# Narrow attention heads on quarters of the array, four heads' scores issued for two steps at once, and the copies of transposed probabilities moved to the front of a step

## What is computed

```python
x = ln(x + attn0(x))                    # 16 heads of 64, one extra key and value of zeros
x = ln(x + xattn0(x, ctx, mask))        # 16 heads of 16, keys with mask 0 are left out
x = ln(x + moe(x))                      # 8 experts, two per token
x = ln(x + ssm(x))                      # 4 layers of a selective scan
x = ln(x + xattn1(x, ctx))              # own block with 8 heads of 32, and a feed-forward part
x = ln(x + bitlinear_ffn(x))
```

## Time and profile before

| what | value |
|---|---|
| median of 3 runs | 4847.31 us (4841.17 to 4852.92) |
| profiled execution | 4848.16 us |
| its span | 4846.5 us |
| PE busy | 83% of the span |
| DVE busy | 65% |
| ACT busy | 48% |
| POOL busy | 47% |
| granted PE clock, mean | 0.935 |

### The profile page before, as it was taken

How to read it: one execution, slowest core, us unless ns; L and a number is a source line. 1 busy time by engine, 2 the same in 40 slices (tenths; PEclk the granted TensorE clock), 3 DMA queues, 4 the chain that set the end, 5 groups by cost and what they waited for, 6 DMA issues and landing times.

```text
span 4846.5 us, 47769 instructions
## 1 busy us (share of the span) xinstructions
PE 3999.0 (83%) x14984; PEld 2038.4 (42%) x14992; DVE 3135.2 (65%) x4273; ACT 2329.8 (48%) x4232; POOL 2281.4 (47%) x1206
## 2 busy tenths in 40 slices
PE   7888888888869995888888888888888966676766
PEld 3433443444449992233333333333333323333333
DVE  3555446446541112699999998999899995554454
ACT  4444445435422223666666666666666542232332
POOL 2344334324410004678777787778777773120210
PEclk9999999999979997899999999999999998887988
DMA  6000000000058882011111111111111120000000
GB/s 208 18 5 10 18 13 2 18 14 9 1 197 316 310 321 86 22 36 33 45 34 37 31 45 33 38 33 45 33 38 33 33 65 33 1 13 13 0 5 4
DMA packets 102370, 272.71 MB, mean 56 GB/s; under 512 B 9776, under 2 KB 55728, under 8 KB 96400
## 3 DMA queue, kind: packets, MB, share of 16 engines
q1 hardware_dynamic: 97216, 256.75, 15.6%
q0 software_dynamic: 4944, 13.51, 0.8%
HBM read 237.32 MB, written 32.90 MB: 56 GB/s over the span
## 4 chain that ended last, share of the span: by engine, by line
PE 54%; DVE 15%; POOL 15%; issue 11%; ACT 3%; SPq 1%; DMA 1%; DVEq 0%; POOLq 0%; ACTq 0%
POOL AR L706 10%; PE PS L1319 6%; PE PS L1112 6%; PE PS L1095 6%; PE PS L1083 6%; PE PS L1208 6%; PE PS L1059 5%; DVE AR L1760 5%; PE PS L1067 4%; PE PS L1264 4%; PE PS L1218 3%; DVE PS L1754 3%; PE PS L1235 2%; POOL AR L664 1%; ACT AR L769 1%
## 5 line engine op out<-in xcount | busy, mean ns | idle before, releaser
L706 POOL TENSOR_TENSOR AR<-AR 128x1024 f32<-128x1024 f32 x512 | 1212.7, 2370 | 520.5 <-DVE AR L1760 520.4
L605 POOL TENSOR_TENSOR AR<-AR,rden 128x1024 f32<-128x1024 f32 x320 | 605.7, 1893 | 1292.0 <-DVE rden L1523 1225.8
L1319 PE MATMUL PS<-AR,ident 128*128 128x512 f32 x2048 | 1034.4, 629 | 195.7 <-POOL AR L706 195.6
L1760 DVE TENSOR_TENSOR_SCAN AR<-AR,PS 128x1024 f32<-128x1024 f32 x512 | 1170.3, 2286 | 17.6
L968 ACT ACTIVATE AR<-AR,mcol 128x511 f32<-128x511 f32 x1024 | 664.9, 711 | 143.1 <-DVE AR L1760 139.5
L1754 DVE TENSOR_TENSOR PS<-AR,PS 128x1024 f32<-128x1024 f32 x512 | 627.9, 1226 | 143.3 <-PE PS L1305 127.7
L1319 PEld LDWEIGHTS PS<-AR,ident 128*128 128x128 f32 x2048 | 367.6, 194 | 680.3 <-issue 341.4
L1095 PE MATMUL PS<-ident,AR 128*128 128x128 f32 x2560 | 345.2, 278 | 124.4 <-issue 67.1
L1095 PEld LDWEIGHTS PS<-ident,AR 128*128 128x128 f32 x2560 | 276.8, 142 | 383.7 <-issue 363.5
L1083 PE MATMUL PS<-AR 64*128 64x512 f32 x1280 | 365.0, 651 | 52.0 <-ACT AR L769 23.0
L769 ACT ACTIVATE AR<-PS,nm 128x512 f32<-128x512 f32 x384 | 260.1, 683 | 282.2 <-DVE nm L1503 217.0
(11 more groups left out here) (265 smaller groups left out, 4798.3 us busy)
## 6 DMA issues: line engine op xcount, KB each, us to landing
AR<-in_xw SPq DMA_DIRECT2D x39, 3072.0 KB, 10.4
AR<-mid_cs SPq DMA_DIRECT2D x256, 256.0 KB, 3.3
mid_xs<-AR SPq DMA_DIRECT2D x32, 512.0 KB, 8.0
AR<-mid_xs SPq DMA_DIRECT2D x39, 128.0 KB, 9.5
mid_ys<-AR POOLq DMA_DIRECT2D x39, 128.0 KB, 8.0
AR<-in_ctx SPq DMA_DIRECT2D x8, 512.0 KB, 5.1
AR<-in_mask SPq DMA_DIRECT2D x4, 1024.0 KB, 5.2
mid_x<-AR SPq DMA_DIRECT2D x8, 512.0 KB, 3.0
```

The costliest lines, as they stand in the source:

```text
L605: pool.tensor_tensor(probs[:, i % 4], probs[:, i % 4], rden[:, i % 4, :].rearrange("p (q o) -> p q o", o=1).to_broadcast([P, 2, 512]), ALU ...
L706: pool.tensor_tensor(m_HC[:, W % 3], m_H[:, W % 3, :].rearrange("p (c s) -> p c s", c=2), m_cb[:, n % 4:n % 4 + 1, :].to_broadcast([P, 2, ...
L1319: ins = pe.matmul(PS[:, 2 * hf + c, :], ident[:], m_HC[:, W % 3, c, :], start=False, stop=n == NS - 1)
L1760: v.tensor_tensor_scan(m_H[:, W % 3, :], m_dA[:, W % 4].rearrange("p c s -> p (c s)"), PS[:, 4:6, :].rearrange("p c s -> p (c s)"), 0.0, A ...
```

## The change

For `per` = 4 each head gets its own quarter of the array. The projected queries are kept once, so `pj_q`, the second copy and the small tables behind it go. One step still takes two heads, but the order of steps alternates between two pairs of heads, so that steps i and i+1 (i even) hold the four heads of a block for the same queries. PE issues the scores of both steps together, in even steps only, as four matmuls with 32 rows each into four PSUM banks. Before them it waits for step i-1: in B for its `nm` (`smax`), in E for its exponentials (`probs_ok`). AV goes to four matmuls of 256 moving columns on four column quarters, in place of two of 512. In `per` = 4 both DVE and ACT issue the copy of T(i-3) as the first thing of step i. Attention A keeps its order.

```diff
         def head(j, q, per):
-            return 2 * j + q if per == 2 else 4 * (j // 2) + j % 2 + 2 * q
+            return 2 * j + q
+
+        def step_of(i, per):
+            return (i // T, i % T) if per == 2 else (2 * (i // 8) + i % 2, i % 8 // 2)
...
# ACT
                 for i in range(n + LAG):
+                    if i >= LAG and per == 4:
+                        copy(i - LAG)
                     if i < n:
+                        exps(i)
+                    if i >= LAG and per == 2:
+                        copy(i - LAG)
...
                 for c in range(4):
-                    pj_q(b, PJ_BQ + c, b_qT, c, 4, qs_b, qb_b)
+                    pj(b, PJ_BQ + c, b_qT[:, c, :], ACT.Identity, 0.25, cols[:, C_BQ + c:C_BQ + c + 1])
...
# PE
-                        if i >= 2:
-                            pe.wait_ge(probs_ok, s - 1)
-                        for q in range(2):
-                            h = head(i // T, q, per)
-                            r = 64 * q
-                            part = h % 2 * (qT.shape[1] // 2) if per == 4 else 0
-                            ins = pe.matmul(PS[:, 2 * (i % 2) + q, :],
-                                            qT[r:r + 64, part + h // per, t * P:(t + 1) * P],
-                                            kT[r:r + 64, h // per, :], start=True, stop=True)
-                        ins.then_inc(scores, 1)
+                        free = smax if masked else probs_ok
+                        if per == 2 and i >= 2:
+                            pe.wait_ge(probs_ok, s - 1)
+                        if per == 4 and i % 2 == 0 and i >= 2:
+                            pe.wait_ge(free, s)
+                        for e in ((i,) if per == 2 else (i, i + 1) if i % 2 == 0 else ()):
+                            j, t = step_of(e, per)
+                            for q in range(2):
+                                h = head(j, q, per)
+                                r = h % per * wide
+                                ins = pe.matmul(PS[:, 2 * (e % 2) + q, :], qT[r:r + wide, h // per, t * P:(t + 1) * P],
+                                                kT[r:r + wide, h // per, :], start=True, stop=True)
+                            ins.then_inc(scores, 1)
...
-                        for q in range(2):
-                            h = head(j, q, per)
-                            p0 = h % per * wide
-                            ins = pe.matmul(PS[p0:p0 + wide, 6 + bank % 2, :], V[:, c, h * wide:(h + 1) * wide],
-                                            pT[j % 2][:, q, c, :], start=c == 0, stop=c == 3)
+                        for q in range(per):
+                            h = per * bank + q
+                            p0 = q * wide
+                            n0 = 0 if per == 2 else u % 2 * 256
+                            moved = (pT[u % 2] if per == 2 else
+                                     pT[u % 2].rearrange("p a c n -> p (a c n)").rearrange("p (h c n) -> p h c n", h=4, c=4))
+                            ins = pe.matmul(PS[p0:p0 + wide, 6 + bank % 2, n0:n0 + 1024 // per], V[:, c, h * wide:(h + 1) * wide],
+                                            moved[:, q, c, :], start=c == 0, stop=c == 3)
...
# DVE
                 for i in range(n + LAG + 5):
                     s = s0 + i
+                    if per == 4:
+                        copy(i - LAG)
                     if i < n:
...
-                    k = i - LAG
-                    if 0 <= k < n:
-                        v.wait_ge(pt_ps, s0 + k + 1)
...
+                    if per == 2:
+                        copy(i - LAG)
```

More of the change, by code:

```diff
@@ L376, in head, with part_of @@
         def head(j, q, per):
-            return 2 * j + q if per == 2 else 4 * (j // 2) + j % 2 + 2 * q
+            return 2 * j + q
+        def step_of(i, per):
+            return (i // T, i % T) if per == 2 else (2 * (i // 8) + i % 2, i % 8 // 2)
+        def part_of(pT, k, q, per):
+            j, t = step_of(k, per)
+            if per == 2:
+                return pT[k // 4 % 2][:, q, :, t * P:(t + 1) * P]
+            quad = pT[k // 4 % 2].rearrange("p a c n -> p (a c n)").rearrange("p (h c n) -> p h c n", h=4, c=4)
+            return quad[:, 2 * (j % 2) + q, :, t % 2 * P:(t % 2 + 1) * P]
         def kmaj(a):
@@ L744, in pj @@
                 act.activation(dst, PS[:, u % 4, :], func, bias=bias, scale=scale).then_inc(pj_ev, 1)
[L746 to L753, removed]
             def ln(b, i):
@@ L757, in ln, with attend, exps, copy @@
                 act.activation(std[:], mv[:, :, 1], ACT.Sqrt, bias=epsc[:, 0:1]).then_inc(ln_std, 1)
-            def attend(b, at, n, src, zero_key, probs, pT):
+            def attend(b, at, n, src, per, probs, pT):
                 s0, g0 = AT(b, at), GT(b, at // 4)
+                def exps(i):
+                    s = s0 + i
+                    act.wait_ge(smax, s + 1)
+                    if i >= 4:
+                        act.wait_ge(pt_ps, s - 3)
+                        act.wait_ge(den_ok, s - 3)
+                    for q in range(2):
+                        ins = act.activation(probs[:, i % 4, q, :], src(i, q), ACT.Exp,
+                                             bias=nm[:, i % 4, q:q + 1], accum_out=sm[:, i % 4, q:q + 1])
+                    if per == 2:
+                        ins = act.activation(e0[:, i % 4, :], nm[:, i % 4, :], ACT.Exp)
+                    ins.then_inc(probs_ok, 1)
+                def copy(k):
+                    act.wait_ge(pt_ps, s0 + k + 1)
+                    if k % 4 == 0 and k >= 8:
+                        act.wait_ge(av, g0 + k // 4 - 1)
+                    act.activation(part_of(pT, k, 1, per), PS[:, 5, :].rearrange("p (c q) -> p c q", q=P), ACT.Copy).then_inc(pt_a, 1)
@@ L771, in attend @@
-                        if zero_key:
-                            ins = act.activation(e0[:, i % 4, :], nm[:, i % 4, :], ACT.Exp)
-                        ins.then_inc(probs_ok, 1)
-                    k = i - LAG
[L775 to L780, removed]
+                        exps(i)
@@ L1013, in _ @@
                 for c in range(KC):
-                    pj_q(b, PJ_EQ + c, s_qT, c, KC, qs_e, qb_e)
-                attend(b, AT_E, 16, lambda i, q: PS[:, 2 * (i % 2) + q, :], False, e_probs, e_pT)
+                    pj(b, PJ_EQ + c, s_qT[:, c, :], ACT.Identity, 32.0 ** -0.5, cols[:, C_QB + c:C_QB + c + 1])
+                attend(b, AT_E, 16, lambda i, q: PS[:, 2 * (i % 2) + q, :], 4, e_probs, e_pT)
                 ln(b, 5)
@@ L1069, in tm, with attend @@
                 ins.then_inc(tm_ps, 1)
-            def attend(b, at, n, qT, kT, V, per, ot, probs, pT, between=None):
+            def attend(b, at, n, qT, kT, V, per, ot, masked, probs, pT, between=None):
                 s0, g0, o0 = AT(b, at), GT(b, at // 4), OT(b, ot)
@@ L1101, in attend @@
                     if x >= 0:
-                        j, c = x // 4, x % 4
-                        bank = j if per == 2 else j // 2
+                        u, c = x // 4, x % 4
+                        bank = u if per == 2 else u // 2
                         if c == 0:
-                            pe.wait_ge(pt_a, s0 + 4 * j + 4)
-                            pe.wait_ge(pt_v, s0 + 4 * j + 4)
+                            pe.wait_ge(pt_a, s0 + 4 * u + 4)
+                            pe.wait_ge(pt_v, s0 + 4 * u + 4)
                             if bank >= 2:
                                 pe.wait_ge(o_sb, o0 + bank - 1)
-                        for q in range(2):
-                            h = head(j, q, per)
-                            p0 = h % per * wide
-                            ins = pe.matmul(PS[p0:p0 + wide, 6 + bank % 2, :], V[:, c, h * wide:(h + 1) * wide],
-                                            pT[j % 2][:, q, c, :], start=c == 0, stop=c == 3)
+                        for q in range(per):
[6 more added lines that the diff above has]
+                                            moved[:, q, c, :], start=c == 0, stop=c == 3)
                         if c == 3:
@@ L1420, in _ @@
             v.wait_ge(ld_const, 64)
-            for g in range(4):
-                for k in range(2):
-                    v.memset(strip01[32 * g:32 * g + 32, k:k + 1], 1.0 if g % 2 == k else 0.0)
             v.wait_ge(act_set, 1)
@@ L1433, in _ @@
             v.wait_ge(r_init, 5)
[L1434 to L1438, removed]
+            v.sem_inc(dve_set, 1)
             v.wait_ge(dve_set, 1)
@@ L1484, in attend, with copy @@
                 s0, g0 = AT(b, at), GT(b, at // 4)
+                def copy(k):
+                    if not 0 <= k < n:
+                        return
+                    v.wait_ge(pt_ps, s0 + k + 1)
+                    if k % 4 == 0 and k >= 8:
+                        v.wait_ge(av, g0 + k // 4 - 1)
+                    v.tensor_copy(part_of(pT, k, 0, per), PS[:, 4, :].rearrange("p (c q) -> p c q", q=P)).then_inc(pt_v, 1)
                 for i in range(n + LAG + 5):
                     s = s0 + i
```

(2 more changed lines are left out.)

24 lines of the change are left out of this document (6 added, 18 removed).

## The result

The changed kernel takes 4922.41 us (median of 4 runs, 4919.67 to 4923.54), the kernel before 4846.52 us in the same comparison: a ratio of 1.0155, with a 95% interval of 1.0138 to 1.0173. It is slower by about 76 us. The forecast was 4848.8 us, with a range from 4830 to 4895; both were wrong.

What follows compares the result with a forecast made beforehand. The prediction took B and E to be bound by a mostly latency loop through all engines, not PE's busy time. B -26.0, E +22.0 and d +4.6 made +0.6 on 4848.16, so 4848.8 us, range 4830 to 4895.

Steps and rivals of the forecast that it cites:

- Part 1: PE work in B and E: four quarters at once and halved AV take 1.0 us a step off PE.
- Part 5: Scores in B and E: whether four quarters cost more than two; 4.6 us added in all.
- d: Extra time of four-quarter scores over two, 92 times in B and E: taken 0.05 us, bounds 0 and 0.86.
- Part 2: New order's loops, two steps: B 6.66 us against 6.99, E 7.49 against 6.34.
- The joints behind a copy: In the loops of B and E, from DVE's copy to its next pass: 0.65 us.
- Part 3: Whole phases with beginning and end: B 111.9 us, 5.8 less; E 63.3 us, 6.2 more.
- the cancellation: B's gain and E's loss over four phases each, -26.0 and +22.0 us with Part 4, nearly cancel.
- the sum: Whole kernel: B -26.0, E +22.0, d +4.6, together +0.6 us on the profiled 4848.16.
- Part 4: Projections before each of eight phases: one activation less saves 0.7 us each; set-up saves nothing.
- The clock drops: Rival: PE's idle time in E's new loop halves the clock; 55 us more, 4904; chance 0.10.
- The first rival: Scores' quarters don't all run at once: one extra pass 4884 us, pairs one behind the other 4923; chance 0.20.

Runs made afterwards that it cites:

- step_ramp_filled: scores_by_step plus two unread full-size products in each of the first seven steps of B and E; 4794.74 us, ratio 0.9879.
- filled_gaps: The changed kernel plus two unread products of 128 rows and 512 columns in each even step of B and E, before its wait; 4837.81 us, ratio 0.9972.
- gaps_filled_narrow: filled_gaps with its two unread products on 32 rows of the array in place of 128; 4917.92 us, ratio 1.0131.
- pairs_copies_last: The changed kernel with both copies moved back to the end of the step, pairs of steps and quarters kept; 4863.24 us, ratio 1.0023.
- scores_by_step: The changed kernel with one step's scores issued at a time, behind a wait for step i-2; quarters and copies first kept; 4784.6 us, ratio 0.9864.

## Why the prediction was wrong

Point by point, by the prediction's own steps:

- *Part 1, four quarters at once, and Part 5, d.* Right: S to T 1.07 us against 1.06, so d is about 0.01 (0.05 taken). The halved AV takes 0.57 us to the next instruction instead of 0.98, so it saves 0.4 and not 0.5. The count of 92 in Part 5 is a little high, since it has 15 of the 16 even steps of a B and all 8 of an E; with d near nothing this costs nothing. The span model of the page "TensorE: Matmul & The Clock Gate" of the Trainium skill (section "Part 3: Packing small matmuls — row/col tiling"), a few ns for each tile more, agrees with this 0.01. The d of 0.32 that the prediction worked out from the page's 3.07 is not there, but that does not refute the 3.07: the prediction applied it to a length in which two tiles already ran together. Two full products one behind the other take 1.81 us in step_ramp_filled, so four would take 3.6 (an estimate), 3.4 times the 1.07 of the four quarters.
- *Part 2, the loops.* Right as an order, and near in size at 2.4 GHz: B 6.45 to 6.49 us for two steps against 6.66, E 7.50 to 7.59 with the gaps filled against 7.49. The joints behind a copy are 0.61 rather than 0.65. DVE's wait for T and PE's wait before S stand where the prediction put them.
- *Part 3, whole phases.* Right at the full clock (109.7 and 65.6 against 111.9 and 63.3, from filled_gaps, whose products delay S slightly), and with them the cancellation: over all eight phases B and E together come out 0.9 us longer than before, and filled_gaps ends 5 to 13 us below the kernel before, where the sum had 0.6 above.
- *Part 4, 0.7 us before each phase.* Not resolved. Between A and B the changed kernel is 0.6 to 1.8 us shorter than the kernel before, but filled_gaps, with the same projections, is anything from 0.8 shorter to 0.5 longer.
- *The rivals.* This is the step that failed: the sum prices every link at a granted clock of 1.00, and the changed kernel ran B at 0.87 to 0.88 and E at 0.69 to 0.79. "The clock drops" was named, placed in E, and given a chance of 0.10. It is what happened. The evidence against it was a stretch of the scan at 52% busy and 1.00. That compared busy shares, and the runs show that busy time does not decide: filled_gaps and gaps_filled_narrow give PE instructions of the same length and number, and on one chip they differ by 69 us. The scan's products use all 128 rows; the changed kernel's scores use 32 for each head. The work removed in Part 1 was counted as time won on PE only, and its second effect, on the clock, was not asked about.
- *Its price.* 55 us over 28 even steps of E, none in B. The 28 is miscounted: only the six steps 4 to 14 of each E have both scores and a transpose, which by the same pieces makes 47. Measured in the E of batch 1: two steps cost 1.8 to 2.7 us more than forecast (9.32 to 10.20 us, at mean clocks of 0.50 to 0.68) rather than 1.96, the beginning and the end of E suffer too (78.2 against 63.3, 14.9 a phase), and B loses its gain (117.5 to 119 against 111.9) in its first 20 us and in single later stretches. Against the forecast, E is 55 us over and B 24; 5 of d were not needed, A is 1 longer and the rest 4 shorter than its share. That makes 71, by which the profiled execution (4919.67) lies above 4848.8.
- *A number that came true by luck.* The first rival, pairs one behind the other, was priced at 4923, and 4922.41 was measured. Its sign, T 1.5 or 1.9 us behind S at the full clock, is not there: the 2.01 in E belongs to the lower clock, and at 1.00 it is 1.07.

Left open: how the low level comes about inside E, and why one B of gaps_filled_narrow stays up. What the runs show is a contrast between kernels, not the rule by which the chip decides. The quarters alone bring the clock down to 0.78 in most E phases; that the late wait and the copies take it further, to 0.69, is seen, but why is not. That pairs_copies_last needs 115 to 120 us for B was not followed up either.

## What to carry to other kernels

Work taken off an engine that mostly waits is worth only what the loop through all engines gives back: write down that loop, put the moved waits into it, and look at what is queued behind each. Before packing products into smaller tiles, ask what the granted clock will do when less of the array is fed, and read it after: a kernel with fewer PE passes came out 76 us slower through it, and the best version here left the scores on halves, with zeros in the queries. When parts of a change are bundled, time them apart: copies first alone gained 1.0%, quarters alone lost 0.3%, and together with the pairs they lost 1.55%.

## What was not expected of the hardware

- The granted clock can stay at 1.2 GHz while PE shows as busy all the time: 16 us in scores_by_step, at 8.00 of 8 us busy.
- Two unread products with 128 rows in each pair of steps held B at 1.00 and E at 0.95 to 0.97; the same two with 32 rows, equally long, left E at 0.77 to 0.81 and three B at 0.86 to 0.89, while the fourth B was at 0.98.
- The same scores on two tiles of 64 rows, half of the query rows zeros, against two tiles of 32 rows: 1.00 against 0.77 in E, with steps of B equally long at the full clock.
- Four tiles of 32 rows took as long as two of 64 (1.07 and 1.06 us to the next instruction), and the eight AV records of four products of 256 columns on four column tiles 0.64 us, against 1.05 for the four of two products of 512 on two. (So a product of 256 columns shows as two records, like one of 512; it is the transposes that show as one.)
